# A graph kernel's sorting front: clearing only the padding rows, 16-bit histogram one-hots, tile tables built inside the scatter

## The reference, cut to what matters

```
h        = relu(layernorm(x))                                  # 3125 x 128
message  = leaky_relu(concat(h[dst], edge_attr) @ w1 + b1)      # per edge
hidden   = segment_sum(message, src)                            # per node, then @ w2, the update network
# three more layers (attention with relation weights, GCN, mean aggregation) use, per edge,
# the count and the relation weight of (src, dst): sums over the same edge list
```

## Time and profile before

| What | us |
|---|---|
| median of 3 runs | 3380.41 (3377.36 to 3380.56) |
| the profiled execution | 3380.8 |
| its span, first to last instruction | 3379.1 |
| front block | 0 to about 181 |
| POOL's first scatter | 280.19 |
| last scatter issued | 1310.5 |
| first instruction of the edge stage | 1318.8 |

### The profile page before, as it was taken

One profiled execution on the slowest core, in us unless ns is written; L12 is line 12 of the kernel. 1 busy time (PEld: TensorE's weight loads), 2 busy tenths in 40 slices (PEclk: granted clock), 3 DMA queues, 4 the chain that ended last, 5 costly groups with the idle time before them and its releaser, 6 DMA issues. The chain is left out here.

```text
span 3379.1 us, 87741 instructions
## 1 busy us (share of the span) xinstructions
PE 2511.1 (74%) x20390; PEld 1974.6 (58%) x20391; DVE 2597.0 (77%) x8325; ACT 1489.4 (44%) x3942; POOL 1952.3 (58%) x2344
## 2 busy tenths in 40 slices
PE   1433555555555554999999999999999239989899
PEld 1322334333334343999999999999997214445455
DVE  7863777777777773999999999999997779983501
ACT  2011222222222222677777777777775655452200
POOL 1005777777777777899999999999996000000000
PEclk9975677677777776999999999999999559999999
DMA  9993222222222223888888888888886669869766
GB/s 381 414 414 129 78 78 83 78 78 78 77 79 78 78 68 104 236 240 234 242 239 235 240 239 234 242 238 236 241 239 226 255 282 343 301 219 315 249 220 208
DMA packets 738172, 696.84 MB, mean 206 GB/s; under 512 B 48524, under 2 KB 637275, under 8 KB 734779
## 3 DMA queue, kind: packets, MB, share of 16 engines
q1 hardware_dynamic: 516770, 536.77, 47.6%
q10 hardware_dynamic: 195544, 104.71, 12.7%
q0 software_dynamic: 25792, 54.52, 4.9%
HBM read 340.91 MB, written 354.90 MB: 206 GB/s over the span
## 5 line engine op out<-in xcount | busy, mean ns | idle before, releaser
L855 POOL DMA_INDIRECT sorted_rows<-rows,posi x806 | 785.1, 974 | 338.7 <-issue 221.4
L1147 DVE SCALAR_TENSOR_TENSOR acc<-acc,keep,pm 128x256 f32<-128x256 f32 x1504 | 715.7, 476 | 70.9 <-issue 23.9
L965 POOL TENSOR_SCALAR ohs_e<-iota,rt 128x128 f32<-128x128 f32 x1128 | 666.2, 607 | 12.4 <-DMA rt<-sorted_rows 12.4
L803 PE MATMUL s_peq<-sb_w1bb,eT 128*128 128x256 f32 x806 | 352.5, 531 | 398.9 <-ACT eT L658 379.9
L1074 PE MATMUL pm<-ohw_e,ohs_e 128*128 128x128 f32 x3008 | 609.1, 283 | 0.0
L974 POOL TENSOR_TENSOR hid<-pre_e,excess 128x512 f32<-128x512 f32 x376 | 482.8, 1284 | 117.2 <-ACT excess L1001 117.2
L1080 PE MATMUL px<-PN,dT 128*128 x4512 | 498.1, 219 | 0.4 <-ACT dT L1014 0.4
L1020 ACT ACTIVATE ohw_e<-ohd_e,rt 128x128 f32<-128x128 bf16 x1504 | 490.5, 397 | 0.0
L1074 PEld LDWEIGHTS pm<-ohw_e,ohs_e 128*128 128x128 f32 x3008 | 461.8, 194 | 0.0
L803 PEld LDWEIGHTS s_peq<-sb_w1bb,eT 128*128 128x128 f32 x806 | 172.8, 265 | 441.1 <-ACT eT L658 432.7
L1091 PE MATMUL ps<-hid,ohs_e 128*128 128x129 f32 x3008 | 424.3, 283 | 0.5 <-POOL hid L974 0.5
(11 more groups left out here) (317 smaller groups left out, 4206.3 us busy)
## 6 DMA issues: line engine op xcount, KB each, us to landing
count_matrices<-acc SPq DMA_DIRECT2D x1504, 128.0 KB, 2.6
sorted_rows<-zrow SPq DMA_DIRECT2D x188, 528.0 KB, 10.5
rt<-sorted_rows ACTq DMA_DIRECT2D x184, 528.0 KB, 4.6
gab<-count_matrices SPq DMA_DIRECT2D x60, 1280.0 KB, 6.0
arb<-count_matrices SPq DMA_DIRECT2D x25, 1664.0 KB, 8.8
ab<-count_matrices SPq DMA_DIRECT2D x25, 1600.0 KB, 9.3
arb<-count_matrices SPq DMA_DIRECT2D x25, 1536.0 KB, 8.5
ef<-in_edge_attr_dram SPq DMA_DIRECT2D x58, 364.0 KB
```

Source lines behind the costliest of these rows:

```text
L803: nc.tensor.matmul(pe_q[:, q % 2, 0:2 * D], eT[:, q % 2, :], w1bb[:], start=True, stop=True).then_inc(s_q, 1)
L855: pool.indirect_dma_start(sortd, bass.IndirectOffsetOnAxis(ap=posi[:, h, c:c + 1], axis=0), rows[:, h, c, :], None).then_inc(s_sc[h], 16)
L965: last = nc.gpsimd.tensor_scalar(ohs[:, k % BUFS, j, :], iota128[:], rt[:, k, j, D + 1:D + 2], None, ALU.is_equal)
L1147: nc.vector.scalar_tensor_tensor(acc[:, k % SUMS, j, :], before, keep[:, at:at + 1] if isinstance(at, int) else keep[:, ds(at, 1)], pm[:, ...
```

## The change

It touches the front and the scatter only; the edge stage and what follows are as they were.

1. **Clearing.** Tiles 0 to 799 (`BLIND` = 100 groups of 8) are no longer cleared blind. The 88 groups behind them still are: 40 in the front, 48 in the scatter block. In tiles 0 to 799 only the padding rows are cleared, by 42 indirect DMAs on POOL. A bin's padding (0 to 128 rows) is cut into blocks of 64, 32, 16, 8, 4, 2 and 1 rows by the bits of its length; for each block size there are 5 DMAs of 125 bins, and an index lies beyond a limit, so that nothing is written, where the bit is not set or the block lies behind tile 800. Two more DMAs of 75 indices clear the unused tiles at the end of each source row. DVE computes the indices in the front (some dozen small operations), and ACT stores them and loads them back to 125 partitions.
2. **One-hots.** The tile numbers and the comparison patterns are 16-bit, and the patterns are stored out in full, so that all three operands step by one element. Chunks have 52 columns (16 chunks). PE reads a column of the one-hots with a step of 52 elements (104 bytes).
3. **Work moved between engines in the front.** HT's copy, the split of the projection and the copies of turned weights go from DVE to ACT and POOL; the bias of the projection becomes a POOL addition in place of a PE product; the projection is done inside the loop over chunks. POOL also converts `lo` and `typ` and adds the bias to X. LayerNorm's statistics come ahead of the indices.
4. **Tile tables.** `tables()` runs on DVE in the scatter, behind `places(0, 1)`, and the transposes and the copies behind them are gone. ACT stores the tables before the last body and loads `keep` and `tilei` at the scatter's end.
5. **Memory.** Several tiles share space with others (`ef` with the tables, `ohL` and `ohT` with H, scratch with S), and `ef` is no longer cleared by POOL.

```diff
-            zrow = sb("zrow", [P, ZR, ROW])
+            zrow = sb("zrow", [P, PADS[0][1], ROW])
+            BLIND = E // P // ZR
+            CLEARED = 40
...
-                SUB = 5 * CH
+                HS = 4
+                SUB = HS * CH
...
-                    with sp.Fori(0, CLEARED) as n:
+                    with sp.Fori(BLIND, BLIND + CLEARED) as n:
...
+                    for n in range(NS):
+                        counts(n)
+                        if 0 <= n - 2 < NQ:
+                            turned(n - 2)
+                        if 0 <= n - 4 < NQ:
+                            projected(n - 4)
+                        if 0 <= n - 5 < NQ:
+                            first(n - 5)
+                        if 0 <= n - 6 < NQ:
+                            second(n - 6)
...
+                    act.wait_ge(s_dv, 4)
+                    act.dma_start(padr.rearrange("k (s d) -> s k d", s=NT), pout[:]).then_inc(s_st, 16)
+                    act.dma_start(fullr, fout[:]).then_inc(s_st, 16)
+                    act.wait_ge(s_st, 48)
+                        act.dma_start(padi[:], padr.rearrange("k (p c) -> p k c", p=PADP)).then_inc(s_pi, 16)
+                        act.dma_start(fulli[:], fullr.rearrange("s (j c) -> (s j) c", c=2)).then_inc(s_pi, 16)
                     act.dma_start(incb[:], rowinc.partition_broadcast(P)).then_inc(s_bo, 16)
...
+                    def bias(g):
+                        nc.gpsimd.tensor_tensor(pr[:, g % 2, 0:k, :], pf[:, g % 2, 0:k, :],
+                                                b1bc[:].unsqueeze(1).to_broadcast([P, k, D]), ALU.add).then_inc(s_pp, 1)
...
-                        nc.vector.tensor_tensor(ohs[:, n % 2, 0:w, :], iota32[:].unsqueeze(1).to_broadcast([P, w, QP]),
-                                                tile[:, 1, c].unsqueeze(2).to_broadcast([P, w, QP]), ALU.is_equal)
+                        nc.vector.tensor_tensor(ohs[:, n % 2, :, 0:w], rep32[:, :, 0:w],
+                                                tile[:, 1, c].unsqueeze(1).to_broadcast([P, QP, w]), ALU.is_equal)
...
-                            nc.tensor.matmul(px[:, g % 2, o:o + D], HT[:, t * P:(t + 1) * P], wl["w1a"][:], start=True, stop=False)
-                            last = nc.tensor.matmul(px[:, g % 2, o:o + D], ones[0:1, :], brow["b1"][:], start=False, stop=True)
+                            last = nc.tensor.matmul(px[:, g % 2, o:o + D], HT[:, t * P:(t + 1) * P], wl["w1a"][:], start=True, stop=True)
...
-                            last = nc.tensor.matmul(hist[QP * j:QP * j + QP, n % 2, o:o + NT], ohs[:, n % 2, c, :],
-                                                    ohd[:, n % 2, c, :], start=True, stop=True)
+                            last = nc.tensor.matmul(hist[QP * j:QP * j + QP, n % 2, o:o + NT], ohs[:, n % 2, :, c],
+                                                    ohd[:, n % 2, :, c], start=True, stop=True)
...
                     places(0, 1)
+                    tables()
                     begin(1, 0, False)
...
-                    nc.gpsimd.memset(ef[:], 0.0).then_inc(s_pad, 1)
-                    nc.gpsimd.memset(rows[:], 0.0).then_inc(s_pad, 1)
-                    pool.wait_ge(s_zd, 16 * (TT // ZR))
+                    nc.gpsimd.memset(rows[:, :, :, D + 3:D + 4], 0.0).then_inc(s_pad, 1)
+                    pool.wait_ge(s_pi, 32)
+                    for k, (bit, size) in enumerate(PADS):
+                        spots = sortd.rearrange("(n s) w -> n (s w)", s=size)
+                        for c in range(BINS // PADP):
+                            pool.indirect_dma_start(
+                                spots, bass.IndirectOffsetOnAxis(ap=padi[:, k, c:c + 1], axis=0),
+                                zrow[0:PADP, 0:size, :].rearrange("p k w -> p (k w)"), None,
+                                bounds_check=BLIND * ZR * P // size - 1, oob_is_err=False).then_inc(s_cl, 16)
...
+                    pool.wait_ge(s_zd, 16 * (TT // ZR - BLIND))
...
+                    act.wait_ge(s_to, 32)
+                    act.wait_ge(s_te, BODIES * PAIRS)
+                    act.wait_ge(s_pos, 2 * BODIES)
+                    act.dma_start(keep[:], tilef[0:TT].partition_broadcast(P)).then_inc(s_tl, 16)
```

More of the change, by code:

```diff
@@ L113, in build @@
         brow = {}
-        for name in ("b1", "bs", "bn"):
+        for name in ("bs", "bn"):
             brow[name] = tsb("row_" + name, [1, D])
@@ L258, in _, with counts @@
                                              scale=rstd[:, t:t + 1]).then_inc(s_ln["h"], 1)
[L260 to L263, removed]
+                    def counts(n):
+                        a, b = n * HS, min(n * HS + HS, NCH)
+                        hv = hist[:, n % 2, 0:4 * HS * NT].rearrange("p (h x) -> p h x", x=4 * NT)
                         act.wait_ge(s_mm, n + 1)
@@ L296, in _ @@
                     line(iotaj[:], [[1, 4], [0, QP]])
+                    line(iota25[:], [[1, NT]])
+                    line(rep32[:], [[1, QP], [0, SUB]])
+                    line(rep25[:], [[1, NT], [0, SUB]])
+                    nc.gpsimd.memset(ident[:], 0.0).then_inc(s_z, 1)
+                    pool.wait_ge(s_z, 3)
+                    nc.gpsimd.affine_select(out=ident[:], in_=ident[:], compare_op=ALU.not_equal, fill=1.0, base=0,
+                                            pattern=[[-1, P]], channel_multiplier=1)
@@ L297, in _ @@
+                    nc.gpsimd.memset(runs[:], 0.0).then_inc(s_con, 1)
+                    line(iota32[:], [[1, QP]])
                     line(edges[:], [[NT, NT]], base=NT)
                     for k in range(3):
-                        line(kidx[:, k, :], [[P, TCOL]], base=k - 1, step=1)
+                        line(kidx[:, k, :], [[1, TCOL]], base=k - 1, step=TCOL)
+                    line(six[:], [[1, 2 * (G - 1)]])
                     line(iotar[:], [[1, NREL]])
                     line(iota128[:], [[1, P]])
-                    nc.gpsimd.memset(later[:], 1.0).then_inc(s_pc, 1)
@@ new lines, in _ @@
+                    nc.gpsimd.memset(PN[:, NT, :, :], 0.0)
+                    pool.wait_ge(s_ld, 16 * 19)
+                    nc.gpsimd.memset(relt[:, 0:1], 0.0)
+                    for g in range(NQ + 1):
+                        if g < NQ:
+                            if g >= 2:
+                                pool.wait_ge(s_pp, third_part[g - 2])
+                            bias(g)
+                            rest(g)
+                        if g >= 1:
+                            third(g - 1)
@@ L505, in _ @@
                     nc.tensor.matmul(wt[:, 3, 0:NT], same[0:NT, :], cnt[:, 4, :], start=False, stop=True).then_inc(s_tp, 1)
-                    for g in range(2, NQ):
-                        project(g)
-                    pe.wait_ge(s_dv, 4)
-                    for k, row in enumerate((0, 1, 3, 2)):
-                        last = nc.tensor.transpose(tt[:, k, :], table[:, row, :], ident[:])
-                    last.then_inc(s_tp, 1)
             with ExitStack() as ctx:
```

380 lines of the change are left out of this document (230 added, 150 removed).

## The result

The changed kernel takes **3460.8 us** (median of 4 runs, 3450.6 to 3464.2) against 3378.9 us before, a ratio of 1.024 with an interval of 1.022 to 1.0259: slower by 82 us, where 3346 us was forecast. The profiled execution took 3464.2 us, 83.4 us more than the one before.

The account below looks back on a forecast made before the run. DMA clearing was taken to bound the time before the first scatter, POOL after it. S = 117 plus 128 us gave F = 245, saving 35.2 us of 3380.8: 3346 us, range 3299 to 3374 us.

Parts of the forecast that it names:

- What bounds the kernel: Whole kernel: DMA clearing is the limit before the first scatter at 280 us, POOL's scatters after it.
- Step 1: Front until the scatter block: clears issued early, the chain of the front sets its end at 117 us, 111 to 133.
- S: Start of the scatter block: 181 us before the change, predicted 117.
- Step 2: Scatter block's start to first scatter: clears, padding and features share the DMA engines, 113 to 140 us, taken as 128.
- rival 2: S to F: padding shared unevenly among DMA engines; F 257 or, on five, 260; 3358 or 3361 us; chance 0.30.
- F: Time of the first scatter: 280.2 us before the change, predicted 245.
- Steps 3 and 4: Scatter: DVE's tables, 35 us, and ACT's loads at the end stay hidden; without cover the loads cost some 5 us.
- Rival 3: POOL pays by the row, not the index: 42 transfers take 968 us, F = 1085, about 4190 us; chance 0.08.
- Rival 4: Nothing gained: PE's column step at its upper end plus uneven sharing, F = 276, 3377 us; chance 0.05.
- Rival 1: Padding doesn't get in the clears' way: F = S + 75 = 192, 3293 us; chance 0.10.

Follow-up runs that it names:

- e8: Changed kernel with all 188 clears blind again (131 in the front, 57 in the scatter block) and no padding transfers: 3375.5 us.
- e13: Changed kernel with the one-hots laid out so that a column's entries are neighbours (PE reads without a step, DVE writes with one): 3630.0 us.
- e12: Changed kernel with POOL's two conversions and its addition to X held back until DVE's scans are done: 3481.3 us.
- e1: Changed kernel with the 42 padding transfers issued behind the last scatter instead of before the first: 3486.8 us.
- e4: Changed kernel without the first five padding transfers, whose 625 indices are all out of range: 3451.6 us.
- e15: Changed kernel with 128 indices per padding transfer, neighbouring bins in a transfer, and all 88 tail clears issued in the front: 3302.5 us, ratio 0.9776.
- e2: Changed kernel with all 88 tail clears issued in the front, none in the scatter block: 3420.8 us.
- e7: Changed kernel, still with 125 indices, with the bins of a padding transfer laid out as neighbours: 3438.7 us.
- e10: The kernel of e15 with 127 instead of 128 indices in each of the 40 padding transfers: 3747.0 us.

## Why the prediction was wrong

**What bounds the kernel** was read rightly: the first scatter came 83.2 us later and the end 83.4, and in the kernel before the clears were the limit (e8).

**Step 1** gave S = 117, range 111 to 133; it is 123.6. The one-hots came out at 1.03 and 0.83 us for 0.94 and 0.75. PE's step, for which I took no cost, doubled the products, 0.57 to 1.18 us (e13); the weight load of the earlier trace rows was too far off to show it. By the Trainium skill (Advanced Engine Details and Errata, section Memory Cachelines: a penalty where each access is to another 16-byte line) it was to be expected. Here trace and rule agree. But this did not reach S. Four projections take 1.06 us and not 2.9, so PE was through ten chunks at 65 us (74 predicted), and then it waits for ACT's copies, and ACT for POOL:

```profile
73.98 1.17 PE L560 MATMUL hist<-S 128*32 128x25 f16 x52 [3.95 <-ACT runs L296]
```
```profile
72.25 0.63 ACT L316 ACTIVATE PN<-pr 128x512 bf16<-128x512 f32 x1 [4.27 <-POOL pr L398]
```

This chain, which Step 1 named, set the last counts, copied at 89.9 (predicted 88). The rest is DVE beside POOL, for which I had added 1.5 us: the scans took 21.5 us instead of 14.3, and e12 shows that POOL's addition costs DVE about its 7 us wherever it lies ahead of S. The Trainium skill (SBUF — State Buffer, section "SBUF: two separate sides") calls the pair of ports which the two share an exclusive lock for a whole instruction; the 6.85 us of the cast agree with that.

**Step 2 failed**, at two places of its text. It priced the 42 "if one with 125 indices costs what one with 128 does": for POOL's issuing that is nearly so (1.49 us from start to start, 1.28 with 128), for the DMA engines not at all. And it bounded the bytes between 113 and 140 us by sharing among engines that each move 25.8 GB/s, and took 128 (the middle of 113 and rival 2's 143); from S to F it is 239.8 us. **Rival 2 had the mechanism**: five engines for a transfer of 125, in turn. Its sentence on the Trainium skill (DMA: Bandwidth & Descriptors, section "Why a DMA increments its semaphore by 16 and not by 1") gives the rule, the largest number of engines up to 16 that divides the slowest dimension. The trace agrees with that rule for 125 (share 0.31) and 127 (6.3%, one engine), and with 128 all engines were full (share 1.01 at 414 GB/s). What it lacked is the price of several in flight: 10.8 GB/s for a busy engine in e1 instead of 25.8. Its 143 us would have been too low in any case; with F = 123.6 + 143 the time would be 3367.

The sum closes: F came 118.4 us later than the 245 predicted, 6.6 of it from S and 111.8 from Step 2, and 3345.6 + 118.4 = 3464.0, against 3464.2 measured. The bytes had two smaller faults of their own: the 2.1 MB left out, and features that the sum takes at 2.1 MB where the text gives 1.7.

I also named POOL's wait for clears behind the 42 transfers. There was none, because the queue had filled up first and the padding outlasted the clears; the prediction lists that as a sign that it is wrong. e4 shows that with room in the queue the clears, slowed by the padding, would have held POOL until 354.

**Steps 3 and 4** held: the tables were done on DVE at 187 us, hidden now under a longer wait, POOL kept its pace of 1.28 us, and the edge stage came 9.2 us behind the last scatter. **Rival 3** was wrong in its mechanism: a transfer of 125 costs POOL 1.2 us whether its blocks have one row or 64. **Rival 4** fell with Step 2. **Rival 1** fell too, but its price was right: without padding ahead of it, e1's first scatter came at 196.5, where it said 192 with S 5.6 us earlier.

Left open is why transfers of 125 slow one another. Different engines then read the same partitions of the zero rows at nearly the same time, which would fit; no run changed that alone.

## What to carry to other kernels

Choose the number of indices of an indirect transfer for the DMA engines, and fill up with indices out of range if need be: here 128 instead of 125 brought the first scatter forward by 77 us, and 127 instead of 128 cost 448 us. Price a queue by what its transfers do to the DMA engines, not by what the issuing engine spends on them, and lay the indices that count evenly over the partitions. Issue early what can be early: the same clears in an idle stretch of the front, together with these two, turned a loss of 82 us into a gain of 76 (e15).

## What the runs showed of the hardware that was not expected

- POOL's queue took 39 transfers of 125 indices before it stood still (the changed kernel, e1, e2 and e7 alike), seven of 127, and all 42 of 128. And it took no more until all of these had been moved: in the changed kernel the queue's last packet ended at 357.9 and the fortieth transfer began at 359.4, in e1 at 1398.3 and 1399.8, in e10 at 346.2 and 347.1.
- A transfer makes packets that move no rows: an empty one of 125 indices 416 (e4), which is 16 x 26, and the first seven of 127, five of them empty, 14,336 together (e10), which is 7 x 16 x 128. An estimate from these counts: if each of the 16 engines has a list, and a transfer of 125 adds 26 entries to each and one of 127 adds 128, then 39 x 26 = 1014 and 7 x 128 = 896 fit, and 40 x 26 = 1040 and 8 x 128 = 1024 do not.
- A 16-bit compare on DVE that writes with a step of 64 bytes takes 7.40 us for 1664 elements; one that writes neighbours and leaves the step to PE takes 1.03.
